# A second, early row buffer and two scatters in the head of a two-layer graph kernel

## What is computed

```python
# layer 0; W1..W4 are chosen by the node's type (2), W5 by the edge's type (3)
h1, h2, h3, h4 = (proj(x, Wk, bk, node_type) for k in 1..4)
w5e   = einsum(edge_attr_16, W5[edge_type]) + b5[edge_type]
num   = sum(h3[dst] * (h4[src] + w5e), axis=-1)
score = softmax((num / sqrt(16))[:, None], axis=-1)   # over an axis of length one
x = layernorm(x + h1 + segment_sum(score * (h2[src] + w5e), dst))
# layer 1
m   = relu(x[src] + edge_attr_32 @ We + be) + 1e-7
a   = segment_softmax(m, dst)                          # per channel
agg = segment_sum(m * a, dst)
x = layernorm(x + (x + agg) @ Wm + bm)
```

## Time and profile before

| what | value |
|---|---|
| runs | 2236.8, 2242.93, 2247.61 us; median 2242.93 |
| the profiled execution's own time | 2247.74 us |
| its span, first to last instruction | 2245.8 us |
| mean granted TensorE clock | 0.886 of full speed |
| busy: PE, PE weight loads, DVE, ACT, POOL | 78%, 49%, 71%, 34%, 58% |
| DMA | 323.65 MB, mean 144 GB/s |

### The profile page before, as it was taken

How to read it: one execution, slowest core, us unless ns; L and a number is a source line. 1 busy time by engine, 2 the same in 40 slices (tenths; PEclk the granted TensorE clock), 3 DMA queues, 4 the chain that set the end, 5 groups by cost and what they waited for, 6 DMA issues and landing times.

```text
span 2245.8 us, 29209 instructions
## 1 busy us (share of the span) xinstructions
PE 1747.1 (78%) x9112; PEld 1108.5 (49%) x9112; DVE 1602.6 (71%) x3058; ACT 757.1 (34%) x1397; POOL 1294.3 (58%) x1348
## 2 busy tenths in 40 slices
PE   6453889898889889888873487888878787878873
PEld 5222556665666556555662144454445444544442
DVE  7422677777777777677768377788778786878786
ACT  3100222222222222222222144455455545455461
POOL 6365555555666565565633666666666665656624
PEclk9876999999999999999986688899999998989885
DMA  8942444545554555454443145555545555545442
GB/s 274 369 96 83 131 137 134 156 134 154 138 150 141 144 145 144 137 146 133 139 133 93 39 117 148 148 161 153 148 147 150 150 148 143 152 144 151 144 151 57
DMA packets 220072, 323.65 MB, mean 144 GB/s; under 512 B 62802, under 2 KB 127948, under 8 KB 219789
## 3 DMA queue, kind: packets, MB, share of 16 engines
q1 hardware_dynamic: 132958, 150.94, 22.9%
q0 software_dynamic: 43056, 68.05, 13.7%
q10 hardware_dynamic: 43904, 102.79, 12.6%
HBM read 188.35 MB, written 133.22 MB: 143 GB/s over the span
## 4 chain that ended last, share of the span: by engine, by line
PE 28%; issue 17%; another core or an unknown queue 16%; ACT 12%; DVE 12%; ACTq 3%; POOL 2%; DMA 1%; DVEq 0%; SPq 0%; POOLq 0%
PE wide L957 8%; PE wide L1069 5%; ACT block L860 3%; PE wide L931 3%; PE wide L966 2%; ACTq L853 2%; ACT prob_wide L837 2%; PE wide L923 2%; ACT msg L838 2%; ACT block L841 1%; DVE h3d L1363 1%; PE bank L1005 1%; ACT block L830 1%; DVE featm L1354 1%
## 5 line engine op out<-in xcount | busy, mean ns | idle before, releaser
L672 POOL DMA_INDIRECT rows<-d_x,idx x588 | 559.7, 952 | 350.2 <-issue 155.3
L662 POOL DMA_INDIRECT block<-d_h,idx x482 | 462.9, 960 | 302.9 <-issue 126.8
L1069 PE MATMUL wide<-late,ntype_i 125*128 125x512 bf16 x975 | 240.4, 404 | 54.7 <-DVE ntype_i L1492 49.5
L662 POOL DMA_INDIRECT rows<-d_h,idx x160 | 153.8, 961 | 151.6 <-PE wide L931 58.3
L1363 DVE TENSOR_TENSOR_SCAN h3d<-keep,h3d,bank 128x512 f32<-128x512 bf16 x98 | 124.9, 1275 | 159.1 <-issue 114.4
L1069 PE MATMUL wide<-edge_lists,ntype_i 125*128 125x512 bf16 x936 | 229.2, 401 | 11.9 <-issue 11.5
L931 PE MATMUL wide<-typed,zeros 128*128 128x128 f32 (+1 forms) x1364 | 185.0, 283 | 13.1 <-issue 13.1
L1080 PE MATMUL wide<-ident,block 128*128 128x128 f32 x784 | 134.4, 320 | 72.0 <-ACT block L860 43.9
L1069 PEld LDWEIGHTS wide<-late,ntype_i 125*128 125x128 bf16 x975 | 101.1, 104 | 176.2 <-DVE ntype_i L1492 49.9
L957 PE MATMUL wide<-late,ntype_i 125*128 125x512 bf16 x702 | 177.1, 409 | 12.5 <-issue 5.0
L957 PE MATMUL wide<-edge_lists,ntype_i 125*128 125x512 bf16 (+1 forms) x702 | 170.7, 396 | 11.6 <-issue 9.2
(11 more groups left out here) (255 smaller groups left out, 3214.2 us busy)
## 6 DMA issues: line engine op xcount, KB each, us to landing
d_run<-block ACTq DMA_DIRECT2D x98, 512.0 KB
d_inj<-zeros SPq DMA_DIRECT2D x28, 896.0 KB
inj<-d_inj SPq DMA_DIRECT2D x98, 256.0 KB
d_run<-stage ACTq DMA_DIRECT2D x98, 256.0 KB
feat<-in_ea16x3T SPq DMA_DIRECT2D x196, 96.0 KB
types<-d_type SPq DMA_DIRECT2D x196, 64.0 KB
keep<-d_keep SPq DMA_DIRECT2D x196, 64.0 KB
keep<-d_pen SPq DMA_DIRECT2D x196, 64.0 KB
```

What stands on the lines that cost most here:

```text
L662: pool.indirect_dma_start(out=ring[c % RING][:, j, h, :], out_offset=None, in_=d_h24, in_offset=bass.IndirectOffsetOnAxis(ap=idx[:, c, at: ...
L672: pool.indirect_dma_start(out=rows1[c % RING1][:, j, h, :], out_offset=None, in_=d_x1, in_offset=bass.IndirectOffsetOnAxis(ap=idx[:, c, at ...
L1069: ins = pe.matmul(p_hot[s], table[q][:, SPLIT * k:SPLIT * (k + 1), :].rearrange("p b c -> p (b c)"), hot[s][:, k, :], start=(k == 0 and q ...
```

## The change

It adds a second DRAM array `d_early` for the rows of chunks 0 to 13 (14 x 1024 rows, 4 zero units) and keeps `d_inj` for chunks 14 to 97 (24 zero units). DVE computes a second list of row numbers, `early_i`: a node whose first edge lies in the early rows goes there, any other to a row behind them.

- SP: the first 7 zero units are 4 of `d_early` and 3 of `d_inj`; 7 more follow with the parts of `d_h24`; the 14 that followed the last part now go out two at a time at the end of the SP work of chunks 2 to 8. A unit is written in pieces of 448 values from a small zero region that is read four times, instead of 1792 from one row. The wait for all zeros ahead of the source numbers is gone. `fix` goes to `d_early`. `load_inj` of chunk 14 waits for both scatters.
- GpSimd: the scatter to `d_early` comes first, ahead of all gathers; it needs only the four early zero units, the projections and the row numbers. The gathers follow from chunk 0. New waits: ahead of chunks 0 and 1 for `looked` of units 0 and 1 (2 and 4), ahead of chunk 2 for the picks of units 0 and 1. The gather of chunk c waits for chunk c-4 up to chunk 7, for c-6 up to chunk 23, and for c-8 from chunk 24. Behind the gathers of chunks 8, 9, 10, 11 and 12 stand five tiles each of the scatter to `d_inj`, after a wait for all zero units.
- Picks: `PICK_LEAD` is 2 instead of 4 and `FIRST_STEP` 0 instead of 3, so that units 2 to 35 are picked in steps 0 to 93, where units 4 to 35 were picked in steps 3 to 90.
- DVE: the break in the row counts is gone; the copy's difference comes behind the row numbers. ACT no longer waits for all zeros, since the weights don't lie in the part of the tile that is still read.

```diff
RING = 8
-AHEAD = 6
 ZEROS = 28
-ZEROS_EARLY = 7
+ZEROS_EARLY = 3
+ZEROS_LATE = 14
+EARLY = 14
+AHEADS = ((24, RING), (RING, RING - 2), (0, RING - 4))
+EARLY_UNITS = 4
+EARLY_ROWS = EARLY * 2 * CH
+SCATTER_BEHIND = {c: (5 * n, 5 * n + 5) for n, c in enumerate(range(8, 13))}
 FIRST = 6
...
 UNITS = -(-PICKS // 2)
-PICK_LEAD = 4
+PICK_LEAD = 2
 PICK_RING = 5
...
 AHEAD_PIECES = len(LEAD_PIECES)
-FIRST_STEP = 3
+FIRST_STEP = 0
 SPLITS = {2: (0, 6, KT), 3: (0, 4, 8, KT)}
...
         d_inj = scratch("d_inj", [EP + P * NT, C])
+        d_early = scratch("d_early", [EARLY_ROWS + P * NT, C])
         d_run0 = scratch("d_run0", [EP + 1, C])
...
         first_i = sb("first_i", [P, NT], i32)
+        early_i = sb("early_i", [P, NT], i32)
         mid_i = sb("mid_i", [NP, 2], i32)
...
         s_rows_i, s_injzero, s_inj = sem("s_rows_i"), sem("s_injzero"), sem("s_inj")
+        s_early = sem("s_early")
         s_fix, s_fixed, s_mbcol, s_mbps, s_mb_i = sem("s_fix"), sem("s_fixed"), sem("s_mbcol"), sem("s_mbps"), sem("s_mb_i")
...
+        def rows_ahead(c):
+
+            return next(ahead for first, ahead in AHEADS if c >= first)
+
+        encoded_by = {c: 2 * c + 2 for c in range(PICK_LEAD)}
+
         def rows_to(c):
...
         of_node = d_h24.rearrange("(p i) c -> p i c", i=NT)
-        row_unit = {4: 0, 5: 1}
-        scatter_unit = {0: 2, 16: 3}
...
             sp.dma_start(idx[:, 0:RING, :], all_idx[:, 0:RING, :]).then_inc(s_idx[0], 16)
-            flat = d_inj[0:EP, :].rearrange("(z p r) c -> z p (r c)", z=ZEROS, p=P)
+            flat, flat_early = (rows.rearrange("(z p a x) c -> z p a (x c)", z=units, p=P, a=4)
+                                for rows, units in ((d_inj[0:EP, :], ZEROS), (d_early[0:EARLY_ROWS, :], EARLY_UNITS)))
+            no_rows = zeros[:, 0:7 * C].unsqueeze(1).to_broadcast([P, 4, 7 * C])
+
+            def clear(first, behind):
+                for z in range(first, behind):
+                    sp.dma_start(flat[z], no_rows).then_inc(s_injzero, 16)
+
             sp.dma_start(x_sb[:, :, :], t["x"].rearrange("(p i) c -> p i c", i=NT)).then_inc(s_types, 16)
...
             sp.wait_ge(s_w24, 32)
-            for z in range(ZEROS_EARLY):
-                sp.dma_start(flat[z], zeros[:, :]).then_inc(s_injzero, 16)
+            for z in range(EARLY_UNITS):
+                sp.dma_start(flat_early[z], no_rows).then_inc(s_early, 16)
+            clear(EARLY_UNITS, EARLY_UNITS + ZEROS_EARLY)
             sp.wait_ge(s_rowlists, 3)
...
             sp.dma_start(wm[C:P, :], t["ident"][C:P, C:P]).then_inc(s_weights, 16)
-            for first, behind, zeroed, zeros_to in ((0, 10, ZEROS_EARLY, 11), (10, 20, 11, 14), (20, NT, 14, ZEROS)):
+            for first, behind, zeroed, zeros_to in ((0, 10, EARLY_UNITS + ZEROS_EARLY, 11), (10, 20, 11, ZEROS_LATE), (20, NT, ZEROS_LATE, ZEROS_LATE)):
                 sp.wait_ge(s_sel, (behind + 1) // 2)
...
                     sp.dma_start(of_node[a:b, first:behind, :], H[a:b, first:behind, C:3 * C]).then_inc(s_h24, 16)
-                for z in range(zeroed, zeros_to):
-                    sp.dma_start(flat[z], zeros[:, :]).then_inc(s_injzero, 16)
+                clear(zeroed, zeros_to)
...
-            def load_inj(s, r, of_inj):
+            def load_inj(s, r, c):
                 wait(sp, injT[s], r)
-                sp.dma_start(inj[s][:, :, :], d_inj[bass.ds(of_inj, 2 * CH), :]
+                if c == EARLY:
+                    sp.wait_ge(s_inj, 2 * 16 * NT)
+                sp.dma_start(inj[s][:, :, :], (d_early if c < EARLY else d_inj)[bass.ds(c * (2 * CH), 2 * CH), :]
                              .rearrange("(p j h) c -> p j (h c)", j=TILES, h=2)).then_inc(inj_in[s], 16)
...
                 load_pick(u)
-            sp.wait_ge(s_injzero, 16 * ZEROS)
             sp.dma_start(idx[:, RING:CHUNKS, :], all_idx[:, RING:CHUNKS, :]).then_inc(s_idx[1], 16)
...
             sp.wait_ge(s_inj, 16 * NT)
-            sp.dma_start(d_inj[1:2, :], fix[0:1, :]).then_inc(s_fixed, 16)
+            sp.dma_start(d_early[1:2, :], fix[0:1, :]).then_inc(s_fixed, 16)
             sp.wait_ge(s_fixed, 16)
             for c in range(2):
-                load_inj(c, 0, c * (2 * CH))
+                load_inj(c, 0, c)
             sp.dma_start(bm_wide, t["bm"].to_broadcast([NP, C])).then_inc(s_fixed, 16)
...
                 s, r = c % 2, c // 2
+                if c == 2:
+                    load_pick(PICK_LEAD + 1)
                 load_features0(s, r, halves(c))
-                load_inj(s, r, c * (2 * CH))
+                load_inj(s, r, c)
                 load_keep(s, r, halves(c))
-                for u in range(PICK_LEAD + 1, UNITS):
+                for u in range(PICK_LEAD + 2, UNITS):
                     if c == max(2, UNTIL[u - LISTS] + 1):
                         load_pick(u)
+                clear(min(ZEROS_LATE + 2 * (c - 2), ZEROS), min(ZEROS_LATE + 2 * (c - 1), ZEROS))
...
                     pool.wait_ge(s_end, 1)
-                if c == 3:
-                    pool.wait_ge(s_shift, 1)
-                if c == 4:
-                    pool.wait_ge(s_mbps, 1)
-                if c == 5:
-                    pool.wait_ge(s_h3, 1)
-                if c in row_unit:
-                    pool.wait_ge(picked[0], row_unit[c] + 1)
-                if c >= RING:
-                    pool.wait_ge(q2_ready[c % 2], (c - RING) // 2 + 1)
+                if c in encoded_by:
+                    pool.wait_ge(looked, encoded_by[c])
+                if c == PICK_LEAD:
+                    pool.wait_ge(picked[0], PICK_LEAD)
+                ahead = rows_ahead(c)
+                if c >= ahead:
+                    pool.wait_ge(q2_ready[c % 2], (c - ahead) // 2 + 1)
                 for h in range(2):
...
+            def scatter(rows, at_row, first, behind):
+
+                for i in range(first, behind):
+                    pool.indirect_dma_start(out=rows, out_offset=bass.IndirectOffsetOnAxis(ap=at_row[:, i:i + 1], axis=0),
+                                            in_=H_all[:, i, 3 * C:4 * C], in_offset=None).then_inc(s_inj, 16)
+
+            pool.wait_ge(s_sel, KT)
+            pool.wait_ge(s_early, 16 * EARLY_UNITS)
+            pool.wait_ge(s_rows_i, 1)
+            scatter(d_early, early_i, 0, NT)
             pool.wait_ge(s_h24, 16 * 6)
-            for c in range(AHEAD):
+            for c in range(CHUNKS):
                 gather0(c)
-
-            pool.wait_ge(s_injzero, 16 * ZEROS)
-            pool.wait_ge(s_rows_i, 1)
-            for i in range(NT):
-                if i in scatter_unit:
-                    pool.wait_ge(picked[0], scatter_unit[i] + 1)
-                pool.indirect_dma_start(out=d_inj, out_offset=bass.IndirectOffsetOnAxis(ap=first_i[:, i:i + 1], axis=0),
-                                        in_=H_all[:, i, 3 * C:4 * C], in_offset=None).then_inc(s_inj, 16)
-            for c in range(AHEAD, CHUNKS):
-                gather0(c)
+                if c in SCATTER_BEHIND:
+                    pool.wait_ge(s_injzero, 16 * (ZEROS - EARLY_UNITS))
+                    pool.wait_ge(s_inj, 16 * NT)
+                    scatter(d_inj, first_i, *SCATTER_BEHIND[c])
...
                 copy_code(u)
-            act.wait_ge(s_injzero, 16 * ZEROS)
+            act.wait_ge(s_zeros, 1)
             for b in range(2):
...
             then(dve.tensor_scalar(first_i[:, :], node_i[:, :], float(DUMP), None, ALU.add))
+            then(dve.tensor_scalar(early_i[:, :], node_i[:, :], float(EARLY_ROWS), None, ALU.add))
...
             for i in range(NT):
-                if i == BOUNDS[3]:
-                    for q in range(3):
-                        then(dve.memset(table[q][:, NT:, :], 0.0))
-                    dve.wait_ge(s_rounded, 1)
-                    dve.tensor_tensor(left0, x_sb[:, :, :], table[0][:, 0:NT, :], ALU.subtract).then_inc(s_left, 1)
                 dve.wait_ge(s_got[group_of(i)], 16 * size(group_of(i)))
...
             dve.wait_ge(s_mbcol, 1)
-            dve.wait_ge(s_rounded, 2)
-            dve.tensor_tensor(table[2][:, 0:NT, :], left0, table[1][:, 0:NT, :], ALU.subtract).then_inc(s_left, 1)
+            for q in range(3):
+                then(dve.memset(table[q][:, NT:, :], 0.0))
...
             then(dve.tensor_tensor(tmp_n[:, :], tmp_n[:, :], in_row[:, :], ALU.add))
-            dve.tensor_copy(first_i[0:NP, :], tmp_n[:, :]).then_inc(s_rows_i, 1)
+            then(dve.tensor_scalar(in_row[:, :], tmp_n[:, :], float(EARLY_ROWS), None, ALU.is_lt))
+            dve.tensor_copy(first_i[0:NP, :], tmp_n[:, :])
+            then(dve.scalar_tensor_tensor(tmp_n[:, :], tmp_n[:, :], float(-EARLY_ROWS), node[:, :], ALU.add, ALU.subtract))
+            then(dve.tensor_tensor(tmp_n[:, :], tmp_n[:, :], in_row[:, :], ALU.mult))
+            then(dve.scalar_tensor_tensor(tmp_n[:, :], tmp_n[:, :], float(EARLY_ROWS), node[:, :], ALU.add, ALU.add))
+            dve.tensor_copy(early_i[0:NP, :], tmp_n[:, :]).then_inc(s_rows_i, 1)
```

(4 more changed lines are left out.)

## The result

The changed kernel takes 2284.24 us (median of 3 runs, 2283.3 to 2286.3) against 2242.93: 41 us more, a ratio of 1.0188 (95% interval 1.0147 to 1.0229). The forecast was 2214. The profiled execution has a span of 2282.4 us, against 2245.8 before.

The account below looks back on a forecast made before the run. Loop bound by PE, with stalls; GpSimd's order sets the head. Chunk 13's scan at 278, plus 857.8, 13.7, 12 and 5, gives 1166.5, 29 us less: 2219 profiled, forecast 2214; 8-in-10 range 2184 to 2258.

Parts of the forecast that it names:

- E0: Start of the `h3d` scan of chunk 0, the loop's first: forecast 120 instead of 202.87, 83 us earlier.
- one late signal: Head: two lead units' products end by about 100, by 108 with a late signal, before chunk 2's turn at 115.
- rival B: Head: lead picks come late during first scatter, GpSimd waits ahead of chunk 2; E0 142, 2236 us; 18 in 100.
- E0 to E7: Loop, scans of chunks 0 to 7, now picking from step 0: 7 x 10.7 = 75 us, ending 195, +6.5.
- E7 to E13: Scans of chunks 7 to 13: GpSimd waits for zeros to 200, then issues for 72 us; ending 278, +21.
- the row with 15.7 us: Old head's trace: `inj` turned by 187.21, the scan waiting for it started at 202.87, 15.7 us later.
- E13 to E97: Loop, scans of chunks 13 to 97: 857.8 us before, plus 13.7, 12 and 5, ending 1166.5.
- E24: Start of the `h3d` scan of chunk 24 in the first loop; the prediction gave it no time of its own.
- three heavy steps at the end: Loop's end: the late three steps now pick, costing 10.39 instead of 5.84 us each, +13.7.
- catching up: Loop: GpSimd starts with one chunk of lead and must catch up; +12 us, bounds 0 and 40.
- rival A: Loop: unbroken GpSimd issue delays what waits for PE, steps last 14.1 us; 2290 at full size; 14 in 100.
- Rival D: Loop: locks make each scatter last as long as the longest gather, 60 us more, 2274; 3 in 100.

Follow-up runs that it names:

- r12: Changed kernel with early array of 35 chunks, second scatter one tile per chunk 11 to 35, lead growing by one, 2.4 us breaks in the head; ratio 1.0082.
- the burst: Kernel before with 25 extra scatters to an unread DRAM array behind the gathers of chunk 40; 2278.62 us, ratio 1.0173.
- the memsets: Kernel before with 64 memsets on GpSimd and no extra DMA behind the gathers of chunk 40; 2268.52 us, ratio 1.015.
- r9: Changed kernel with early array of 28 chunks, second scatter spread over 13 chunks, no last lead raise, five memset breaks of 2.4 us; ratio 1.0027.

## Why the prediction was wrong

Its sum put the last scan of the loop at 1166.5; it came at 1236.59, 70.1 us later. By its own steps:

1. **E0: forecast 120, measured 135.5 (+15.5).** The first scatter started at 66.65 (forecast 65.4). The units of zeros, the order and SP's queue were right: SP issued the loads of `inj` at 109.06, where they were forecast to land at 110. The term that failed is "one late signal" for the lead picks with "chunk 2's turn comes at 115: no cost", as rival B had it. The first scatter and the gathers of two chunks were one run of 54.9 us (66.65 to 121.6), and DVE's next piece of the picks waited for PE until 5 us behind it:

```profile
126.89 0.74 DVE L1345 SCALAR_TENSOR_TENSOR ntype_i<-msg,row_of,wide 64x512 bf16<-64x512 f16 x1 [27.05 <-remote]
```

   GpSimd's own wait ahead of chunk 2 ended at 127.78 for the same reason, and PE turned the waiting `inj` only at 134.22.
2. **E0 to E7: forecast 75, measured 83.2 (+8.2).**
3. **The second scatter and what stands ahead of it, E7 to E13: forecast 83, measured 136.9 (+54).** This is the step of the prediction that failed. It counted GpSimd's 72 us rightly (measured 72.4) and let PE take each chunk as its rows came: E13 was to be 6 us behind the last issue. It came 54.9 us behind it (300.70 to 355.62). But for one wait of 12.0 us, up to 244.11, PE did not lack rows; it and its waiters were held. The bound of 45 us was "five groups that each end in a late signal of 5 us": it took the signal's delay as a fixed addition, where here it lasted 54.0 us, as long as the run that was left and 3.5 us more. In the row with 15.7 us, 10.7 us of the run were left (187.21 to 197.9); the prediction had both numbers and did not put them together. The zeros were a part too: forecast E7 + 5, measured E7 + 9.6 (228.3), behind the `keep` load of chunk 8 at 217.41:

```profile
217.41 1.70 SPq L529 DMA_DIRECT2D keep<-d_keep  x2
220.43 1.31 SPq L470 DMA_DIRECT2D d_inj<-zeros  x2
```

4. **E13 to E97: forecast 888.5, measured 881.0 (-7.5).** The sum is near, its terms are not. From E24 to E97 the loop took 750.2 us against 744.5 before: of the 13.7 us for three heavy steps at the end at most 5.7 came, the steps to chunks 93 and 94 being 6.6 us each (5.8 before), not 10.4. From E13 to E24 it took 130.8 us against 113.3, of which some 14 were the step at chunk 19, where the lead is raised (forecast for catching up: 12). GpSimd's run there:

```profile
406.37 0.95 POOL L682 DMA_INDIRECT block<-d_h,idx  x1 [2.43 <-PE wide L955]
...
430.38 0.94 POOL L682 DMA_INDIRECT rows<-d_h,idx  x1 [0.30 <-issue]
```

   The text had called the limited lead a source of pauses ("against" rival A). It is the other way round at each raise.

5. **The second layer**: 1045.8 us behind the last scan, 1050.6 before: all but unchanged, as forecast.

Rival A named the mechanism, its place and the point from which it decides (E13 later than 307; it was 355.6) and gave 2290, 6 us from the time. It was given 14 in 100. That its total is so near is luck in part: its terms over the forecast were 24 us in the steps 1 to 7, 24 at the scatters and 28 more behind chunk 13, where 8, 54 and some 5 were measured, and it had nothing of the 15.5 us at E0. What stood against it, "the new waits and the limited lead make pauses", was read from the code, while the three late rows were from the trace. Had the delay of 15.7 us been set beside the 10.7 us for which GpSimd still went on, A would have deserved more; the late row to 163.40, which ended in the middle of a run, would have stood against the simple form of it. Rival B came true in part: the lead picks were held and GpSimd waited ahead of chunk 2, but E0 is 135.5, not 142. Rival D fell: the 25 scatters of the loop have a median of 972 ns and a longest of 1358. A lock shows in the first scatter: four of its 25 took 1.77, 1.93, 4.38 and 1.67 us instead of 0.97, some 6 us in all, the first two beside DVE's subtractions (L1309, L1320), the others beside its list comparisons (L1354). The Trainium skill, "SBUF — State Buffer", section "Who interferes with whom", has DVE in a two-port mode and GpSimd lock each other out for a whole instruction; the trace agrees for the scatter of 4.38 us, from 76.06 to 80.44 beside comparisons that ended at 80.32. The same section says that "PE and ACT never wait on anyone". That may hold of the ports; of the engine as this trace shows it, with 5.61 us of work in 50 beside GpSimd's issues, it would mislead.

## What to carry to other kernels

Measure how long GpSimd issues DMAs without a break, not only how much of its time is taken: from 343 to 1143 us in the kernel before, runs of at most 10.0 us went with ordinary steps, though signals of PE came up to 6.4 us late, and runs of 25 us and more with a step of 24 to 67 us. Don't expect that spreading alone pays: 25 scatters, one a chunk, still cost 1.0 us each. Whatever makes GpSimd late (a wait, a wider lead, work that is moved there) can be paid for a second time in the catch-up run. Raising the lead by small steps was tried once, in r12, and did not pay by itself. And when a trace shows several late waits of one kind, set each beside the length of what ran meanwhile before bounding it by the largest one seen.

## What the runs showed of the hardware

While GpSimd issues indirect DMAs 0.30 us apart, results of PE reach ACT and DVE late, up to 54.0 us (250.19 to 304.18). In the changed kernel PE's own matmuls thin out to one in 1.4 to 3.5 us, 24 us into the run; in the burst and behind the memsets it begins some 10 us in. Memsets on GpSimd for 37.87 us do neither. 2.4 us of memsets between issues ended the hold in the loop, 0.6 us did not, and in the head of r9 2.4 us did not either. In the longest runs of the changed kernel, of the two kernels without the second scatter, of r9 and of the burst every recorded signal of ACT and DVE (few: 9 in the changed kernel's) came within 0.01 us of its instruction's end. What is shared between PE and GpSimd's issuing isn't shown by any run: the DMA engines are at 0.12 to 0.18 in it. Nor is it shown why some signals pass in the middle of a run, or why single scatters spread over the chunks cost 1.0 us each.
